# Decoder layer on one core: batch 1's first projections ahead of the first attention unit, three buffers for rows, GpSimd-issued key copies, and a new written order

## The reference, cut to what matters

```python
# x: (4, 256, 256) float32, ctx: (4, 256, 256)
x = layernorm(x + attention(x))                  # 32 heads of 8, 8 key/value heads, softmax over 256 keys
x = layernorm(x + wkv(w, u, k=x, v=ctx))         # a scan over 256 tokens, state p, q, o
x = layernorm(x + ffn(x))
# attention: Q = x@Wq+bq, K = x@Wk+bk, V = x@Wv+bv; softmax(Q K^T / sqrt(8)) V @ Wo + bo
# wkv step: no = max(o, u+k); y = (exp(o-no) p + exp(u+k-no) v) / (exp(o-no) q + exp(u+k-no)); then the state decays
# ffn: y = relu(x@up)^2 @ down + (x@expert) * (sum of the top 2 of x@gate); layernorm(y)*gamma + beta
```

## Time and profile before

| | |
|---|---|
| three runs | 216.08, 217.32, 217.39 us, median 217.32 |
| profiled execution | 216.79 us |
| its span, first to last instruction | 215.0 us |
| mean granted TensorE clock | 0.991 |
| busy share PE, DVE, ACT, POOL | 93%, 76%, 70%, 60% |

### The profile page before, as it was taken

The page is one execution under the profiler, slowest core; times in us unless marked ns, Lnnn a source line. Parts: engine busy times, 40 slices in busy tenths (PEclk is TensorE's granted clock), DMA queues, the critical chain, the costliest instruction groups (busy, mean ns, idle before and its releaser), DMA issues.

```text
span 215.0 us, 4364 instructions
## 1 busy us (share of the span) xinstructions
PE 199.7 (93%) x1295; PEld 111.7 (52%) x1295; DVE 163.1 (76%) x392; ACT 150.9 (70%) x334; POOL 129.6 (60%) x256
## 2 busy tenths in 40 slices
PE   8889999979999899999999999999999998799970
PEld 3533543433433334575465445664655487698950
DVE  3469778778999899998979899976754837956274
ACT  2310477867899789989799879998967984763520
POOL 8995164753465724567476786867495493177622
PEclk9999999999999999999999999999999999999996
DMA  3145227943116602131000000010000000000001
GB/s 122 43 117 170 70 56 226 255 127 108 27 44 203 218 2 64 49 90 36 19 9 7 2 0 9 2 33 25 2 6 0 3 24 26 2 5 0 24 24 49
DMA packets 14759, 12.35 MB, mean 57 GB/s; under 512 B 3856, under 2 KB 12688, under 8 KB 14480
## 3 DMA queue, kind: packets, MB, share of 16 engines
q1 hardware_dynamic: 14064, 11.72, 19.0%
q10 hardware_dynamic: 672, 0.36, 0.6%
HBM read 6.57 MB, written 1.05 MB: 35 GB/s over the span
## 4 chain that ended last, share of the span: by engine, by line
PE 71%; DMA 8%; DVE 7%; ACT 6%; issue 5%; ACTq 1%; POOL 1%; POOLq 0%; DVEq 0%
PE ps_b L781 10%; PE ps_heads L629 10%; PE ps_exp L613 10%; PE ps_b L764 9%; DMA q_rows<-max_t 7%; PE ps_max L600 6%; PE ps_exp L635 4%; PE ps_exp L764 3%; PE ps_b L747 3%; PE ps_a L722 3%; PE ps_a L676 2%; ACT probs L812 2%; PE ps_a L665 2%; DVE maxima L1180 2%; PE ps_a L585 2%
## 5 line engine op out<-in xcount | busy, mean ns | idle before, releaser
L1180 DVE TENSOR_REDUCE maxima<-ps_max 128x2 f32<-128x512 f32 x128 | 85.0, 684 | 10.6 <-PE ps_max L600 9.7
L812 ACT ACTIVATE probs<-ps_exp 128x512 f32<-128x512 f32 x128 | 73.6, 599 | 14.6 <-PE ps_exp L613 14.1
L613 PE MATMUL ps_exp<-q_rows,k_rows 64*128 64x512 bf16 x128 | 46.2, 385 | 3.8 <-ACT probs L812 1.7
L600 PE MATMUL ps_max<-k_rows,q_rows 64*128 64x256 bf16 x256 | 47.4, 274 | 0.7 <-DMA q_rows<-q_parts 0.6
L613 PEld LDWEIGHTS ps_exp<-q_rows,k_rows 64*128 64x128 bf16 x128 | 11.4, 93 | 45.0 <-ACT probs L812 25.9
L629 PE MATMUL ps_heads<-probs,v_cols 128*32 128x512 f32 x256 | 33.9, 604 | 0.0
L781 PE MATMUL ps_b<-down_sb,inner_t 128*128 128x256 f32 x112 | 29.4, 388 | 0.7 <-ACT relu_t L943 0.7
L764 PE MATMUL ps_b<-x_t,up_sb 128*128 128x128 f32 x192 | 27.1, 285 | 1.1 <-DVE h L1367 1.1
L1061 POOL TENSOR_TENSOR rstd<-var_eps,minus_half 128x1 f32<-128x1 f32 x32 | 19.6, 611 | 11.7 <-DVE var_eps L1154 11.7
L764 PEld LDWEIGHTS ps_b<-x_t,up_sb 128*128 128x128 f32 x192 | 23.2, 191 | 6.0 <-issue 4.0
L781 PEld LDWEIGHTS ps_b<-down_sb,inner_t 128*128 128x128 f32 x112 | 19.4, 190 | 4.3 <-issue 1.5
(11 more groups left out here) (129 smaller groups left out, 345.2 us busy)
## 6 DMA issues: line engine op xcount, KB each, us to landing
q_rows<-q_parts SPq DMA_DIRECT2D x46, 64.0 KB, 2.1
x_t<-in_x_cols SPq DMA_DIRECT2D x4, 256.0 KB, 3.3
x_in<-in_x SPq DMA_DIRECT2D x4, 256.0 KB, 4.5
ctx_t<-in_ctx_cols SPq DMA_DIRECT2D x4, 256.0 KB, 3.0
up_sb<-in_up_w SPq DMA_DIRECT2D x1, 1024.0 KB, 6.1
down_sb<-in_down_w SPq DMA_DIRECT2D x1, 1024.0 KB, 6.1
out_y<-y_out SPq DMA_DIRECT2D x8, 128.0 KB, 1.7
post_sb<-in_w_post SPq DMA_DIRECT2D x1, 906.0 KB, 5.5
```

The costliest lines, as they stand in the source:

```text
L600: last = nc.tensor.matmul(ps_max[n % 2][:, r, :], q_rows[b][at:at + HALF, g, REP * jj + 2 * half + r, h * P:h * P + P], k_rows[b][at:at + ...
L613: nc.tensor.matmul(ps_exp[n % 2][:, :], k_rows[b][at:at + HALF, JH * g + jj, kt * P:kt * P + P], q_rows[b][at:at + HALF, g, REP * jj:REP * ...
L812: nc.scalar.activation(probs[n % 8][:, :], ps_exp[n % 2][:, :], ACT.Exp, scale=SCALE).then_inc(s_exp, 1)
L1180: nc.vector.tensor_reduce(maxima[s % 2][:, g, j // JH, 0, at:at + 2], ps_max[n % 2][:, :, :], AX, ALU.max, negate=True).then_inc(s_max, 1)
```

## The change

- **Ramp.** `x_t[1]` is loaded as the third transfer instead of after the ramp. Batch 1's `k` and `q0` run before maxima unit 0 (ticks 1618 and 1820, before 2315 and 2379). The three waits with 16 idle matmuls ahead of unit 0 go. Three idle matmuls each follow `k[1]`, `v[0]` and `q1[0]`.
- **Copies of batch 0.** GpSimd issues the three key copies of parts 1 and 2, between its memsets. ScalarE issues the three query copies of parts 1 and 2 of set 0; SyncE issued one of them before.
- **Rows.** There are three buffers each for `q_rows` and `k_rows` (`ROT = 3`), so batch 3 uses batch 0's. Its copies wait until exp unit 31 is done, and the rows above the maxima are zeroed by one more copy for each set. VectorE clears `q_rows[1]`, GpSimd `q_rows[2]`.
- **`probs`** has 12 buffers instead of 8.
- **Group 0's maxima** are split on GpSimd and copied on ScalarE (both VectorE before). `vb[0]` moves from VectorE to ScalarE.
- **The negated mean** (24 instructions) moves from GpSimd to VectorE, behind `var_eps`.
- **Order.** Nearly all ticks are new. The big loads move among the maxima copies on SyncE's queue.

```diff
-        "k": (1456, 2315, 2440, 3400),
+        "k": (1474, 1618, 2440, 3368),
-        "q0": (1503, 2379, 2792, 3624),
+        "q0": (1520, 1820, 2792, 3688),
-        "kv": (-1, 2342, 2463, 3423),
+        "kv": (-1, 1678, 2463, 3391),
-        "vc": (1610, -1, -1, -1),
+        "vc": (1588, -1, -1, -1),
-        "qh1": (1803, 2716, 3023, 4019),
+        "qh1": (1811, 2640, 3021, 3653),
-        "ql1": (1885, 2922, 3110, 4538),
+        "ql1": (1894, 2827, 3176, 4720),
-        "vb": (1903, 2623, 2687, 4223),
+        "vb": (1795, 2719, 3231, 4127),
-        "kc1": (1634, 2637, 3618, 4606),
+        "kc1": (-1, 2739, 3478, 3836),
-        "kc2": (1703, 2805, 3852, 4658),
+        "kc2": (-1, 2838, 3462, 4785),
-        "qc02": (1737, 2830, 3655, 4911),
+        "qc02": (1762, 2549, 3312, 4871),
-        "qc10": (1831, 2869, 3550, 4417),
+        "qc10": (1989, 2675, 3381, 4901),
-        "qc11": (1931, 2937, 3184, 4896),
+        "qc11": (1894, 2902, 3328, 4615),
-        "qc12": (1989, 3087, 3963, 4919),
+        "qc12": (1962, 2872, 3522, 4760),
-        "load": (2110, 2145, 2179, 2324, 2683, 2857, 3075, 3295, 3839, 3867, 3910, 3941, 3993, 4675),
+        "load": (2165, 2199, 2234, 2860, 2941, 3075, 3094, 3192, 3561, 4179, 4347, 4840, 4886),
-        "m1": (2510, 3026, 3515, 4078, 4571, 5080, 5627, 6178),
+        "m1": (2510, 3018, 3566, 4050, 4572, 5155, 5661, 6186),
-        "mc0": (2311, 2785, 3329, 3804, 4393, 4880, 5290, 5906),
+        "mc0": (2287, 2796, 3297, 3808, 4334, 4852, 5374, 5906),
-        "mc1": (2534, 3055, 3532, 4102, 4591, 5104, 5640, 6183),
+        "mc1": (2534, 3039, 3590, 4094, 4602, 5162, 5672, 6191),
-        "op": (3176, 4104, 4439, 4781, 5224, 5704, 6194, 6796),
+        "op": (3304, 3944, 4424, 4680, 5175, 5736, 6194, 6933),
-        "x1": (3470, 4281, 4687, 4913, 5423, 5871, 6279, 7042),
+        "x1": (3506, 4174, 4613, 4911, 5519, 5871, 6276, 7202),
-        "top0": (3487, 4379, 4735, 4926, 5439, 5885, 6300, 7092),
+        "top0": (3647, 4223, 4799, 4959, 5598, 5949, 6291, 7269),
-        "yt": (4399, 4900, 5368, 5543, 6121, 6383, 7103, 7700),
+        "yt": (4371, 4975, 5574, 5636, 6107, 6529, 7026, 7843),
-        "up1": (4712, 5128, 5768, 5874, 6592, 6902, 7513, 8069),
+        "up1": (4744, 5384, 5874, 5960, 6544, 6885, 7445, 8176),
-        "up2": (4771, 5255, 5607, 5928, 6686, 7259, 7465, 8163),
+        "up2": (4840, 5544, 5768, 6024, 6655, 7240, 7493, 8224),
-        "down0_0": (4872, -1, 6152, -1, 6996, -1, 7866, -1),
+        "down0_0": (5032, -1, 6180, -1, 6980, -1, 7858, -1),
-        "down0_3": (4967, -1, 6201, -1, 7176, -1, 8210, -1),
+        "down0_3": (5167, -1, 6216, -1, 7156, -1, 8035, -1),
-        "h3": (4959, 5567, 6222, 6373, 7233, 7830, 8268, 8535),
+        "h3": (5151, 5726, 6243, 6371, 7213, 7807, 8110, 8561),
...
-    LOAD_AFTER = (0, 0, 0, 0, 20, 28, 0, 0, 0, 44, 0, 0, 0, 0)
+    LOAD_AFTER = (0, 0, 0, 20, 28, 0, 0, 0, 44, 0, 0, 0, 0)
...
+    ROT = 3
+    NPROBS = 12
...
+        def krows_landed(engine, b):
+            engine.wait_ge(s_krows[b], 16 * (len(BLOCKS) if b else PARTS))
+            if b == 0:
+                engine.wait_ge(s_krows_pool, 16 * PARTS)
...
+            def rows_free(b):
+                sp.wait_ge(s_ones, ROT + (b >= 2))
+                if b == 1:
+                    sp.wait_ge(s_q1_zero, 1)
+                if b >= ROT:
+                    sp.wait_ge(s_exp, UNITS * TT * (b - ROT + 1))
...
+            sp.dma_start(flat(x_t[1][:, :, :]), x_cols[1]).then_inc(s_xt[1], 16)
...
-                        for done, value, n_idle in ((s_q2[0], 1, ROW_FILL), (s_q3[0], 1, 6 * ROW_FILL),
-                                                    (s_krows[0], 16 * len(BLOCKS), ROW_FILL)):
-                            pe.wait_ge(done, value)
-                            for k in range(n_idle):
-                                idle_matmul(ident_bf)
...
+                        if b == 1:
+                            for k in range(FILL):
+                                idle_matmul(ident_bf)
...
+            for b in range(1, ROT):
+                gp.memset(k_rows[b][:], 1.0).then_inc(s_ones, 1)
...
+            gp.wait_ge(s_ones, 1)
+            for kp, done in ((1, s_k2), (2, s_k3)):
+                gp.wait_ge(done, 1)
+                k_row_copies(gp, 0, kp, s_krows_pool)
+            gp.memset(q_rows[2][:], 0.0).then_inc(s_ones, 1)
...
-                            if p < WIDE:
-                                gp.tensor_scalar(neg_mean[k][:, ti], mean_var[k][:, ti, 0], -1.0, None,
-                                                 ALU.mult).then_inc(s_negmean[k], 1)
...
+                if p < WIDE:
+                    nc.vector.tensor_scalar(neg_mean[k][:, ti], mean_var[k][:, ti, 0], -1.0, None,
+                                            ALU.mult).then_inc(s_negmean[k], 1)
...
+            nc.vector.memset(q_rows[1][:], 0.0).then_inc(s_q1_zero, 1)
```

More of the change, by code:

```diff
@@ L263, in decoder_layer @@
         k_rest, v_t = [kv[0:KVD] for kv in kv_rest], [kv[KVD:2 * KVD] for kv in kv_rest]
-        q_rows = [sb(f"q_rows{b}", [P, NSET, HH, T], bf16) for b in range(B)]
-        k_rows = [sb(f"k_rows{b}", [P, NSET * JH, T], bf16) for b in range(B)]
+        q_rows = [sb(f"q_rows{i}", [P, NSET, HH, T], bf16) for i in range(ROT)]
+        k_rows = [sb(f"k_rows{i}", [P, NSET * JH, T], bf16) for i in range(ROT)]
         v_cols = [sb(f"v_cols{b}", [P, TT * NSET, GS * 32 + HS]) for b in range(B)]
@@ L275, in decoder_layer @@
         max_t = sb("max_t", [P, NSET, P], bf16)
-        probs = [sb(f"probs{i}", [P, REP * P]) for i in range(8)]
+        probs = [sb(f"probs{i}", [P, REP * P]) for i in range(NPROBS)]
         heads_t = [sb(f"heads_t{i}", [P, REP * P]) for i in range(2)]
@@ L505, in load @@
             def load(j):
-                tiles = ((x_t[1], x_cols[1], s_xt[1]), (x_in[0], x[0], s_x[0]), (ctx_t[0], ctx_cols[0], s_ctx[0]),
+                tiles = ((x_in[0], x[0], s_x[0]), (ctx_t[0], ctx_cols[0], s_ctx[0]),
                          (x_t[2], x_cols[2], s_xt[2]), (post_sb, w_post, s_w_post), (up_sb, up_w, s_up),
@@ L534, in _ @@
                                 else:
-                                    sp.wait_ge(s_ones, 2 * b + 1)
+                                    rows_free(b)
                                 sp.wait_ge(done[g], b + 1)
+                                if b >= ROT and qp == 0:
+                                    sp.dma_start(row_block(q_rows[b % ROT][:, g], len(BLOCKS)),
+                                                 row_block(q_rows[1][:, g], len(BLOCKS) + 1)).then_inc(s_rows[b][g], 16)
                                 q_row_copies(sp, b, g, qp)
-                                if b == 0 and g == 0:
-                                    sp.wait_ge(s_q2[0], 1)
-                                    q_row_copies(sp, 0, 0, 1, (1,))
-                for j in range(14):
+                for j in range(13):
                     if AT["load"][j] == tick:
@@ L600, in maxima_unit @@
                     last = nc.tensor.matmul(ps_max[n % 2][:, r, :],
-                                            q_rows[b][at:at + HALF, g, REP * jj + 2 * half + r, h * P:h * P + P],
-                                            k_rows[b][at:at + HALF, JH * g + jj, :], start=True, stop=True)
+                                            q_rows[b % ROT][at:at + HALF, g, REP * jj + 2 * half + r, h * P:h * P + P],
+                                            k_rows[b % ROT][at:at + HALF, JH * g + jj, :], start=True, stop=True)
                 last.then_inc(s_max_mm, 1)
@@ L629, in pv_group @@
                     last = nc.tensor.matmul(ps_heads[s % 2][32 * j:32 * j + 32, :], flat(v_cols[b][:, :, :])[:, at:at + 32],
-                                            probs[(4 * n + j) % 8][:, :], start=(i == 0), stop=(i == 2 * NSET - 1))
+                                            probs[(4 * n + j) % NPROBS][:, :], start=(i == 0), stop=(i == 2 * NSET - 1))
                 last.then_inc(s_pv, 1)
@@ L678, in _ @@
                             last.then_inc(s_q0 if b == 0 else s_a, 1)
+                            if b == 0 and g == 1:
+                                for k in range(FILL):
+                                    idle_matmul(ident_bf)
                     if AT["v"][b] == tick:
@@ L809, in _ @@
                     act.wait_ge(s_exp_mm, n + 1)
-                    if n >= 8:
-                        act.wait_ge(s_pv, (n - 8) // 4 + 1)
-                    nc.scalar.activation(probs[n % 8][:, :], ps_exp[n % 2][:, :], ACT.Exp,
+                    if n >= NPROBS:
+                        act.wait_ge(s_pv, (n - NPROBS) // 4 + 1)
+                    nc.scalar.activation(probs[n % NPROBS][:, :], ps_exp[n % 2][:, :], ACT.Exp,
                                          scale=SCALE).then_inc(s_exp, 1)
-                for kp, done in ((1, s_k2), (2, s_k3)):
-                    if AT[f"kc{kp}"][0] == tick:
-                        act.wait_ge(s_ones, 1)
```

(17 more changed lines are left out.)

104 lines of the change are left out of this document (48 added, 56 removed), and 152 rows, old and new, of the table AT.

## The result

The time went from 216.70 us (median of 16 runs) to 217.86 (median of 16, 216.47 to 218.93): a ratio of 1.0056, 95% interval 1.0037 to 1.0074. The forecast was 214.8, faster; measured is a little slower. The number lies inside the given range and the 1% that I called the same, but the sign is not the one forecast. The profiled execution has a span of 216.5 for 215.0.

The account below looks back on a forecast made before the run. TensorE was taken as the bound after the first attention units, VectorE second. Terms -1.3 + 0.8 - 0.7 - 1.3 = -2.5 gave span 212.5, profiled 214.3, median 214.8 us (-1.2%); range 211.8 to 219.2.

Parts of the forecast that it names:

- Start of unit 0: In the ramp: query copies end at the same moment, 11.7, but the first reduction comes near 14.0 for 13.77: +0.2 us.
- Key copies on GpSimd: In the ramp: GpSimd's key copies, taken at 1.0 us an issue, land near 13, hidden behind the query copies: 0.
- key copies late: Rival: GpSimd waits out VectorE's steps, 2.0 us per issue, first reduction 2.3 later: 217.1 us; chance 0.11.
- Units 0 to 15: Early units: without two projections and splits of maxima, exp unit 0 comes at 23.8 for 24.80: -1.3 us in all.
- Copies of maxima behind loads: SyncE's queue: exp 24 stalls as before, 0; exp 40's copy lands with down_sb near 61: +0.8 us, bounds 0 and +3.2.
- The slower rival: Copies of maxima behind loads: ramp gain lost, exp 24 and exp 40 wait longer: 220.5 us; chance 0.16.
- The old burst's wait: Where the old burst of four loads was, TensorE's wait for a copy of maxima goes: -0.7 us.
- Negated mean: 24 instructions add 3.7 us to VectorE, which has room; GpSimd's chain shortens while TensorE has other work: 0.
- Last chunk: TensorE's new order at the end covers most of the relu stall (0.69) and the h3 stall (1.08): -1.3 us.

Follow-up runs that it names:

- the one-number edit: Changed kernel with down_sb issued just behind, not ahead of, the copy of unit 40's maxima: 213.44 us, ratio 0.984 against the kernel before; repeated, 212.94 us.
- both loads behind: Changed kernel with down_sb behind the copy of unit 40's maxima and up_sb behind that of unit 24's: 215.9 us, ratio 0.9949 against the kernel before.

## Why the prediction was wrong

*Start of unit 0 (+0.2).* 13.55 measured for 14.0; the same code gave 12.52 to 13.68 in the executions profiled, so a term of 0.2 can't be told here. That the query copies end at the same moment was close: 11.2 for 11.7.

*Key copies on GpSimd (0).* The rival "key copies late" fell: 0.58 an issue (0.51 to 0.73), not 2.0, landed in 2.1. Two of VectorE's steps from SBUF to SBUF (8.69 and 9.26) run beside these issues, and neither holds one up by more than 0.2. I called their effect nothing; against ScalarE's queue they gain 0.8 in this order. That the old queue was the last one to end stood in my own working.

*Units 0 to 15 (-1.3).* Right in kind: exp unit 0 at 23.23 for 24.80 (I had 23.8), by unit 24 1.9 ahead, with the spread of about 1 between executions named above. The experiment without the early projections bears out who brings it.

*Copies of maxima behind loads.* For exp 24: a wait of 0.67, in the range of 0.6 to 0.9. For exp 40, **this is the step that failed.** Issue and landing came out: `down_sb` forecast at 54.5 and out at 54.84, the copy forecast to land near 61 and landed at 60.7. What failed is the sentence "Exp unit 40 is due at 61.09 - 1.3 = 59.8". It was ready at 57.5 (60.77 less the wait of 3.30), so the stall of 0.8 became 3.3. Three things make up the 2.3 between.

The first and largest, 1.3, is a misread row. Counted in TensorE's order, where the copy is waited for at units 24 and 40, the matmul at 61.09 that the earlier trace rows and the prediction call exp unit 40's is unit 41's. Unit 40's matmul in the kernel before is this one:

```profile
59.79 0.38 PE L613 MATMUL ps_exp<-q_rows,k_rows 64*128 64x512 bf16 x1
```

ScalarE takes the exp of unit 40 only at 61.40, which hides the difference. So the old copy, issued at 56.10 and by the median landed at 58.0, had 1.8 of cover and not 3.1. With this row the prediction's own working gives 59.79 - 1.3 = 58.5, a landing at 54.5 + 6.1 = 60.6, a wait of 2.1 for 0.8, and a sum of -1.2: too little to be told from no change.

The second, 0.6, is that exp unit 24 came 1.9 earlier (43.74 for 45.61) and not 1.3. The third, 0.4, is work that the new order takes out of the stretch from exp 24 to exp 40. TensorE's projections in it, before (45.6 to 59.78):

```profile
L676 PE MATMUL ps_a<-x_t,qk_sb 128*128 128x256 f32 x8 | 2.3, 405 | 0.0
```

and with the load behind its copy (43.55 to 57.2):

```profile
L691 PE MATMUL ps_a<-x_t,qk_sb 128*128 128x256 f32 x4 | 1.1, 405 | 0.0
```

One projection (1.1 us) now comes after unit 40, and more waits inside the stretch give back most of it: from exp 24 to the moment at which exp 40 is ready it is 13.73 us for 14.18. I had moved the old time by the ramp's forecast gain alone.

The other part of the failure has no term in my sum at all: a wait of 3.3 is followed by TensorE at its low level, 1.6 more. With the 0.2 from the start these are the 5.11 that the one-number edit gives back. My upper bound of +3.2 for this term was about the wait and left out what follows.

*The slower rival* had the right mechanism, the copies of maxima behind loads, and a price made of three losses. Its condition, over 2.5 beyond the forecast, was met by exp 40 alone: 2.5 of wait and 1.6 of clock.

*The old burst's wait (-0.7).* It went. What is left in the kernel with the load behind is at exp unit 24: 0.4 in one trace, and 0.8 in the other, where the copy lands at 43.50 and a reduction ends at 43.53.

*Negated mean (0).* I looked at VectorE's 3.7 us and found room for them, and wrote that GpSimd's shorter chain helped nobody. It is worth 0.6 to 0.9%. The wait that grew fits GpSimd's shorter chain, which ends in an activation that TensorE's transposes wait for; that this is all of it is not shown.

*Last chunk (-1.3).* Half of it came. The relu's wait of 0.7 is gone and that of `h` is 0.4 for 1.1, but `x_t` and `x` have new ones of 0.4 each: 1.1 of waits for 1.8, a gain of 0.7. I had asked only what becomes of the two stalls, and not what the next ones would be on TensorE. From exp unit 127 to the end the span takes 44.9 before and 45.1 after, since 0.8 more of TensorE's work now stands there.

The sum: with exp 40's copy ahead of the load the change gives a ratio of 0.98 to 0.984, 3.5 to 4.2 us. The forecast without its +0.8 for exp 40 is 3.3. That these are near is partly luck: the ramp gave 1.6 to 2.1 in single traces for 1.3, the last chunk 0.7 for 1.3, and the negated mean and the key copies, both put at nothing, gave some. Misplaced by one position, the load turns it into +0.56%.

## What to carry to other kernels

When an order is rewritten, work out again for every transfer both ends: when it lands, and when its user is ready; the second moves with each instruction taken out of the stretch between. Count the units when you read that time off a trace: two neighbours look alike, and one unit was worth 1.3 us here. A large load and a small urgent copy issued within a microsecond of each other should stand in the order of their due times, and putting the small one on another queue doesn't replace that (it left two executions of four late). A stall of TensorE can cost more than its length, so look at the granted clock behind it. Filling a wait with idle matmuls kept the clock here, but won 0.4% of the time, barely beyond the intervals, where moving the load won 2%.

## What the runs showed that I had not expected

- A 32 KB copy issued 0.26 to 0.63 us behind a 1 MB load landed in 5.3 to 5.7 us, on the same queue or on another, 0.2 behind the load; issued 0.64 us ahead of it, it landed in 1.9. On the other queue its packets stood still for 4.1 us.
- After an idle stretch of TensorE of 2.2 to 3.3 us the granted clock fell to 0.50 in six traces of seven: for 3.4 to 6.8 us behind exp 40 (1.6 us lost with 3.4), and in the ramp for 17 us (exp unit 0 7.3 us late). In the seventh, with both loads behind, it stayed at 1.00 after 2.6 us. Without the early projections seven executions of twelve were late.
- GpSimd issued a copy in 0.58 us and it landed in 2.1, no worse than the others.
- A VectorE instruction on one element per partition, with a shortest time of 0.16, took 1.37 beside two GpSimd instructions and 0.72 beside one.
